# A graph network on one core: the node stage's feed-forward taken half by half

## The reference

```python
h = _transformer_conv(h, src, dst, ...)            # edge stage, then gate and skip
h = _layer_norm(h + res, ln_g[i], ln_b[i])
res = h
f = gelu(h @ W1[i].T + b1[i]) @ W2[i].T + b2[i]    # 128 -> 512 -> 128
h = f + res
```

## Time and profile before

| | us |
|---|---|
| median of three runs | 7938.27 |
| the profiled execution, its time | 7866.28 |
| the profiled execution, its span | 7864.5 |
| TensorE matmul busy | 4591.8 (58%) |
| VectorE busy | 4054.1 (52%) |
| ScalarE busy | 2762.9 (35%) |
| GpSimd busy | 3848.5 (49%) |
| node stage of layer 0, in the trace | about 1564.4 to 1650.7 |
| node stage of layer 3, in the trace | about 6316 to 6417 |

### The profile page before, as it was taken

The page is one execution under the profiler, slowest core; times in us unless marked ns, Lnnn a source line. Parts: engine busy times, 40 slices in busy tenths (PEclk is TensorE's granted clock), DMA queues, the critical chain, the costliest instruction groups (busy, mean ns, idle before and its releaser), DMA issues.

```text
span 7864.5 us, 105863 instructions
## 1 busy us (share of the span) xinstructions
PE 4591.8 (58%) x22799; PEld 3687.8 (47%) x22800; DVE 4054.1 (52%) x11127; ACT 2762.9 (35%) x6393; POOL 3848.5 (49%) x4061
## 2 busy tenths in 40 slices
PE   4555555655555556555555565555555655666666
PEld 2444444534444445344444453444444544555555
DVE  4555555645555556455555564555555653333334
ACT  1333333423333334233333342333333432333333
POOL 3555555335555553345555543455555425555553
PEclk6666666676666666766666667666666677878788
DMA  4222222122222222222222222222222211111111
GB/s 127 78 78 74 78 78 77 52 66 76 78 77 79 76 79 57 65 69 77 77 79 77 79 61 68 68 78 78 78 76 80 60 31 44 44 45 45 45 44 27
DMA packets 267185, 536.12 MB, mean 68 GB/s; under 512 B 116251, under 2 KB 148687, under 8 KB 266507
## 3 DMA queue, kind: packets, MB, share of 16 engines
q0 software_dynamic: 180992, 490.24, 23.2%
q1 hardware_dynamic: 78899, 35.89, 1.8%
q10 hardware_dynamic: 6936, 6.69, 0.3%
HBM read 512.41 MB, written 18.03 MB: 67 GB/s over the span
## 4 chain that ended last, share of the span: by engine, by line
PE 27%; another core or an unknown queue 25%; issue 20%; DVE 17%; ACT 5%; DVEq 4%; ACTq 1%; DMA 0%; SPq 0%; POOL 0%; POOLq 0%
PE bank L765 9%; PE bank L784 8%; DVE acc L1191 6%; PE bank L769 2%; PE bank L756 2%; ACT oh L549 2%; DVEq L330 2%; PE bank L805 2%; PE bank L833 1%; DVE alpha L1214 1%; DVEq L1191 1%; DVE slots L1283 1%; DVE oh L1175 1%; PE bank L937 1%
## 5 line engine op out<-in xcount | busy, mean ns | idle before, releaser
L504 POOL DMA_INDIRECT slots<-kv_table,idx x3224 | 3065.0, 951 | 3149.1 <-PE bank L784 1272.7
L784 PE MATMUL bank<-slots,oh 128*128 128x136 f32 (+1 forms) x8060 | 1598.6, 352 | 584.7 <-DVE acc L1191 502.7
L765 PE MATMUL bank<-qs,ohT 128*128 x8080 | 1676.3, 354 | 230.3 <-ACT ohT L540 132.0
L784 PEld LDWEIGHTS bank<-slots,oh 128*128 128x128 f32 x8060 | 1415.4, 253 | 716.9 <-DVE acc L1191 614.8
L765 PEld LDWEIGHTS bank<-qs,ohT 128*128 128x128 f32 x8080 | 1428.7, 256 | 450.4 <-issue 428.3
L1191 DVE TENSOR_TENSOR acc<-acc,bank 128x136 f32 (+1 forms) x4030 | 1173.6, 291 | 603.7 <-PE bank L784 166.4
L1208 DVE TENSOR_TENSOR slots<-slots,bank 128x512 f32<-128x512 f32 x808 | 552.3, 684 | 1312.1 <-remote 1294.4
L540 ACT ACTIVATE ohT<-bank,miss 128x512 f32<-128x512 f32 x1010 | 676.5, 683 | 1360.0 <-PE bank L756 1226.6
L504 POOL DMA_INDIRECT slots<-src_table,idx x806 | 760.8, 944 | 750.5 <-DMA idx<-src_e 233.6
L549 ACT ACTIVATE oh<-iota,rel_e 128x128 f32<-128x128 f32 x3168 | 962.9, 387 | 0.0
L797 PE MATMUL bank<-ident,alpha 128*128 128x128 f32 x204 | 93.7, 459 | 1459.5 <-DVE alpha L1214 1423.0
(11 more groups left out here) (255 smaller groups left out, 4032.7 us busy)
## 6 DMA issues: line engine op xcount, KB each, us to landing
slots<-kv_table,idx POOLq DMA_INDIRECT x3224
kv_table<-slots SPq DMA_DIRECT2D x20, 660.0 KB, 3.4
slots<-src_table,idx POOLq DMA_INDIRECT x806
resets<-flat_len ACTq DMA_DIRECT2D x51, 128.0 KB
idx<-src_e SPq DMA_DIRECT2D x255, 8.0 KB
terms<-flat_rel SPq DMA_DIRECT2D x255, 12.0 KB
resets<-flat_rst SPq DMA_DIRECT2D x2, 1551.0 KB
w<-in_w SPq DMA_DIRECT2D x8, 256.0 KB
```

The lines of the kernel that those rows point to most:

```text
L504: pool.indirect_dma_start(slots[:, k, t, 0:width], None, table, bass.IndirectOffsetOnAxis(ap=idx[:, k, t:t + 1], axis=0))\
L765: mm = pe.matmul(o, ohT[:, j % 2, t, :], qs[:, blocks[j * G + t], 0:HID], start=True, stop=basis is None)
L784: mm = pe.matmul(bank[6 + part % 2][:, o:o + width], oh[:, k % 2, t, :], slots[:, k, t, HID:HID + width], start=True, stop=True)
```

## The change

The first and second products of a group are taken by halves of the columns. The gelus on ScalarE follow the new order (the first half's four, then the second half's four). On TensorE the order for a group becomes: four first products of half 0; in layers 0 to 2 the keys of the group before; then a first product of half 1 and a second product of half 0, four times in turn; in layer 3 the group before is finished here; then the four second products of half 1, with the transposes of the next group after the second of them. The keys of a group begin when the first half of its rows is new, and wait for the second half at block 2. VectorE's program is unchanged, and so is the place of ScalarE's square root behind the eighth gelu.

```diff
             def feed(l, i):
                 for k in range(8):
-                    f, s = k // 2, k % 2
+                    s, f = k // 4, k % 4
...
                     pe.wait_ge(a_ev, START + NB * l + max(m - 1, 0))
+                    if b == 2:
+                        pe.wait_ge(h_new, START + 2 * NI * l + 2 * i + 2 - 2 * NI)
...
-            def expand(l, i):
+            def expand(l, i, s, f):
+                k = 4 * s + f
+                pe.wait_ge(t_out, START + 2 * (NI * l + i) + 2)
+                pe.wait_ge(ffn_act, START + 8 * NI * l + max(8 * i + k - 1, 0))
+                pe.matmul(bank[2 + k % 2][:, 0:HALF], w_1[:, f * HID:(f + 1) * HID],
+                          zT[i % 2][:, s * HALF:(s + 1) * HALF], start=True, stop=True).then_inc(ffn_ps, 1)
+
+            def contract(l, i, s, f):
                 r = NI * l + i
...
+                pe.wait_ge(h_new, START + 2 * r)
+                pe.wait_ge(ffn_act, START + 8 * r + 4 * s + f + 1)
+                mm = pe.matmul(bank[5 + s][:, 0:HALF], w_2[:, f, :], g1[i % 2][:, f, s * HALF:(s + 1) * HALF],
+                               start=(f == 0), stop=(f == 3))
+                if f == 3:
                     mm.then_inc(f2_ps, 1)
+
+            def feed_forward(l, i, last):
+                for f in range(4):
+                    expand(l, i, 0, f)
+                if i > 0 and not last:
+                    finish_group(l, i - 1, last)
+                for f in range(4):
+                    expand(l, i, 1, f)
+                    contract(l, i, 0, f)
+                if i > 0 and last:
+                    finish_group(l, i - 1, last)
+                for f in range(4):
+                    contract(l, i, 1, f)
+                    if f == 1 and i + 1 < NI:
+                        turn_rows(l, i + 1, last)
...
             def finish_group(l, i, last):
                 if not last:
-                    pe.wait_ge(h_new, START + 2 * NI * l + 2 * i + 2)
+                    pe.wait_ge(h_new, START + 2 * NI * l + 2 * i + 1)
                     keys(l + 1, i)
                     return
...
-                expand(l, 0)
-                contract(l, 0, lambda: turn_rows(l, 1, last))
-                expand(l, 1)
-                for i in range(1, NI):
-                    finish_group(l, i - 1, last)
-                    if i + 1 < NI:
-                        contract(l, i, lambda: turn_rows(l, i + 1, last))
-                        expand(l, i + 1)
-                    else:
-                        contract(l, i)
+                for i in range(NI):
+                    feed_forward(l, i, last)
                 finish_group(l, NI - 1, last)
```

More of the change, by code:

```diff
@@ L929, in turn_rows @@
                 mm.then_inc(t_ps, 1)
-            def expand(l, i):
-                r = NI * l + i
[L933 to L949, removed]
-                    mm.then_inc(f2_ps, 1)
+            def expand(l, i, s, f):
[4 more added lines that the diff above has]
+                          zT[i % 2][:, s * HALF:(s + 1) * HALF], start=True, stop=True).then_inc(ffn_ps, 1)
```

## The result

The changed kernel takes 7998.52 us, the median of four runs (7989.78 to 8005.07); beside it the kernel before has 7939.94 us. These medians are 58.6 us apart. The ratio on record is 1.0082, 95% interval 1.0065 to 1.0099, which makes 65 us slower, between 52 and 79. The prediction was 7989.

The account below looks back on a forecast made before the run. TensorE was taken to set the node stages' pace. Loop layers +32 and layer 3 +6 gave +38, the clock +13: +51 us on 7866.28, 7917; with 72 us to the median, 7989 us, range 7950 to 8040.

Parts of the forecast that it names:

- First half's products: Node-stage groups: keys can be issued at +2.9 instead of +5.80, four first products run between second products; 0.7 us won per group.
- Keys earlier: Loop-layer groups: key block 2 waits for VectorE's add, a new 2.1 us standstill, 1.25 us more with `attended(4)`.
- The eighth gelu: Loop-layer groups: late last gelu delays the next root; TensorE stands 2.0 us ahead of the transposes, group 3.4 us longer.
- Groups 0 and 4: First and last groups of a loop layer: group 0 takes 0.7 us more, group 4 takes 1.5 us less.
- The loop layers: Layers 0 to 2, node stages: +10.7 us each, three layers +32 us, before the clock's cost.
- Layer 3: `outputs` 1.64 us later, passed on three times, plus 0.7 and about 0.5 at the end: +6 us.
- The clock: TensorE: 21 new standstills may bring the slow clock, 0 to 2.3 us each; taken as 0.6 each, +13 us.
- Added waits: TensorE, 13 extra waits per group: no cost while a 0.54 us product covers them; without cover, bounded by 13 us.
- Layer starts: Next layer's queries and gathers shift together: taken as 0. Rival, one add either way decides: 7965 or 8013, 9%.
- pure TensorE pace: Rival: root's chain and VectorE's order stay within slack, so TensorE never waits; -12 to -16 us, about 7924; 10%.
- only one standstill shows: Rival: the keys' wait alone or the root's alone costs 15 to 22 us in all, about 7956; 9%.
- The clock at every standstill: Rival: TensorE's clock falls at each new standstill, 38 + 48 = +86 us, 8024; 12%.

Follow-up runs that it names:

- root_keys_mid: Changed kernel, loop layers: next group's root after four gelus, keys between second and third alternating pair; node stages 350.0 us, ratio 1.0020 to the kernel before.
- keys_mid: Changed kernel, loop layers: keys between second and third alternating pair, root still behind the eighth gelu; node stages 373.4 us, ratio 1.0039 to the kernel before.
- root_early: Changed kernel, loop layers: next group's square root between fourth and fifth gelu, keys unmoved; node stages 378.9 us, ratio 1.0053 to the kernel before.
- waits_only: Kernel before with the changed kernel's added TensorE waits, nothing moved; node stages 348.3 us, ratio 1.0006 to the kernel before.
- filled_ahead: Changed kernel, loop layers: three idle products behind key block 1 and three ahead of the transposes; node stages 387.7 us, ratio 1.0079 to the kernel before.
- after_again: The changed kernel, unedited, run again as a control; node stages 397.4 us, ratio 1.0085 to the kernel before.
- after_more: The changed kernel once more, unedited, with more runs, on a fast chip; node stages 396.9 us, ratio 1.0079 to the kernel before.

## Why the prediction was right

Its mechanism and both places were right, and so was the sum over the node stages. That 51 meets 50.6 so closely is in part luck: the loop layers were reckoned 2 us too long and layer 3 1.6 us too short. The execution lost 58.6 us by its medians and 65 by the ratio, so the forecast of 7989 lies just under the lowest of the four runs, and for the rest the prediction has no term. Term by term:

- *First half's products, won 0.7 us a group.* Right: the first keys are at +2.95 (+2.9 predicted), the alternating products 0.54 us each. root_keys_mid, without the two waits, keeps 0.3 to 0.6 of it.
- *Keys earlier, a standstill of 2.1 us, and 1.25 more with `attended(4)`.* 2.09, and 3.28 in that group, 1.19 more. keys_mid takes it away by moving the keys alone.
- *The eighth gelu, 2.0 us.* 1.79 us in the loop layers. root_early takes it away by moving the root alone. An undisturbed middle group is 17.32 us, 3.3 more than before; I had 3.4. The drain that the Trainium skill ("ScalarE: Activation LUTs", What ACT_TABLE_LOAD costs) adds to a table load did not appear: load and root are 1.29 us apart. The sum without the page's figure was the better one.
- *Groups 0 and 4.* Group 0 lost 15.99 - 14.76 = 1.23 us from transposes to transposes in layer 0, and 0.64 and 0.73 in layers 1 and 2, with 0.7 predicted; the last group gained 1.4 to 1.5, with 1.5 predicted.
- *The loop layers:* 32 us and their part of the clock, 18 x 0.6 = 11, made 43; measured are 41.
- *Layer 3:* 6 us and 3 x 0.6 made 8; measured are 9.6. The mis-sized term is the place of `outputs`. I let the fifth first product start at +3.2, behind the third gelu. It starts at +3.42, because in this layer the first wait is 0.59 us and another of 0.17 follows, and with the chain behind it `outputs` is 1.94 us late instead of 1.64. The added waits, which I had put at nothing, make 0.20 of these 0.30 us: waits_only has both gaps and the +3.42 with nothing moved, and its `outputs` is 0.20 us late. An undisturbed group (18.07 us in root_early and keys_mid) is just 1.94 us longer than its 16.13, so all of it passes on, as the prediction said. Three times 0.3 is half of what was missing; the rest, and what the clock costs in this layer, no run separates.
- *The clock, 13 us guessed between 0 and 48.* In the loop layers 9.0 us by filled_ahead, with 11 guessed. What was wrong is the picture behind the guess, half of the standstills paying 1.2 us, so that the size came out near is luck. In the after profile two of three middle groups pay 1.3 to 1.7 us each and the third nothing, and which of them pay changes from layer to layer and run to run (18.95, 20.20, 17.32 in one layer; 19.01, 18.50, 19.02 in another of after_again; 17.31, 19.99, 17.31 in one of after_more, where only one pays). The count of 21 also left out group 0 of the loop layers, whose transposes now wait 1.79 us in layer 0 where they waited 0.17.
- *Added waits, 0:* 0.08 us a group in the loop layers, in the keys; 0.20 us in layer 3, in the products.
- *Layer starts, 0:* within 3 us in the pair on one chip.

Of the rivals, pure TensorE pace fell by the 1.79 and 2.09 us in the profile, and root_keys_mid shows what it would have been: 13.4 to 13.7 us a group. That only one standstill shows fell likewise; keys_mid and root_early are what it would have looked like (373.4 and 378.9 us, 27 and 33 us more than before, not the 15 to 22 that I gave it). The clock at every standstill fell by the undisturbed third groups; but in root_early, with one wait a group, every middle group did pay. The layer starts did not decide.

## What to carry to other kernels

When a step moves on one engine, ask for each engine that it meets what stands *ahead* of the answer in that engine's own order: here a square root behind the last gelu and a bank's reader behind five sums of squares, neither of them moved by the edit. Slack has to be measured against how far the last link moves: 2.6 us of slack and a gelu that starts 6 us later settle the sign before any sum. And move the waiter's neighbours together with it: the same alternation with the keys two pairs later and the root four gelus earlier gives shorter groups than before, though not a time that a whole execution shows.

## What the runs showed of the hardware that I had not expected

*The same program on two other chips takes 5669 and 5667 us instead of 7934 or 7879.* The changed kernel's node stages (396.9 us in sum) and the gathers' issue (0.95 us each) are the same; what differs lies in the stretches in which rows are gathered. The 25 query adds at the start of layer 1, in the changed kernel on the first chip and on the fast one (the earlier trace rows for before):

```profile
L1383 DVE TENSOR_TENSOR qs<-bank,vec_qs x25: 424/425/426, 1700.2 to 1789.2; 128x256 f32<-128x256 f32 x25
```

```profile
L1383 DVE TENSOR_TENSOR qs<-bank,vec_qs x25: 423/425/425, 1197.8 to 1213.2; 128x256 f32<-128x256 f32 x25
```

89 us against 15, with the gathers issued beside them in both. In the edge stages the multiplication that waits for gathered rows:

```profile
L1212 DVE TENSOR_TENSOR slots<-slots,bank 128x512 f32<-128x512 f32 x808 | 552.5, 684 | 1105.0 <-remote 1094.8
```

```profile
L1212 DVE TENSOR_TENSOR slots<-slots,bank 128x512 f32<-128x512 f32 x808 | 551.8, 683 | 90.8 <-DMA slots<-kv_table,idx 86.3
```

1105 us of waiting on the one, 91 on the other. An edge stage takes 1004 to 1030 us there and 1398 to 1499 on the slower chips. What lies behind it was not tried. It does say how a difference of a few tens of microseconds in a node stage is best read: from the stage, not from two whole executions.

*Idle work can shorten a stage.* Three products that nobody reads, ahead of each of two waits, made the node stages 9 us shorter, because the engine's clock stayed at 2.4 GHz (granted clock 1.00). Whole executions did not show the 9 us. The same three products on the other side of the wait made them 14 us longer.
